# The shifted copy of the attention values made by DMA, with new order words for all engines

## Chip, core and metric

The kernel runs on one core of a Trainium2 chip. The metric is the device time of one execution in microseconds (us). TensorE is written PE, VectorE DVE, ScalarE ACT, GpSimd POOL, and SP is the engine that here only issues DMAs.

## What is computed

Sixteen sequences of 512 tokens by 128 channels pass through a state-space block (Mamba: an input projection, a causal convolution, a scan with 16 states for each of 256 channels, an output projection) and then through two layers of local attention with a feed-forward part. Each block has a layer norm ahead of it and behind it, and a residual. All is in float32.

```python
# state-space block
da = jnp.exp(dt_t[:, :, None] * a);  dbu = dt_t[:, :, None] * b_t[:, None, :] * u_t[:, :, None]
state = da * state + dbu;            y_t = jnp.einsum('bds,bs->bd', state, c_t)
...
# local attention, WINDOW = 64, HEADS = 8, DIM_HEAD = 64: each window looks at itself and the one before
def look_around(t):
    p = jnp.pad(t, ((0, 0), (0, 0), (1, 0), (0, 0), (0, 0)))
    return jnp.concatenate([p[:, :, :w], p[:, :, 1:]], axis=3)
bk, bv = (look_around(bk), look_around(bv))
sim = jnp.einsum('bhwid,bhwjd->bhwij', bq, bk)
...
attn = jax.nn.softmax(sim, axis=-1)
out = jnp.einsum('bhwij,bhwjd->bhwid', attn, bv)
```

## The kernel before

**Streams and rounds.** A batch is one sequence. The work on it is cut into streams: E (entry: norm, input projection, convolution), M (the scan of the state-space block: 32 steps, each a 128x512 scan on DVE), A (front: the first attention layer with its feed-forward part, PSUM banks `f_bank`, SBUF tiles with the number 0) and B (back: the second layer, banks `b_bank`, tiles with the number 1), with small streams F, S and C between them. `program` (L1155) runs rounds. In each, M works on batch k+2, A on k+1, B on k and E on k+3, so that in the rounds 0 to 13 all four run side by side. The order in which an engine issues the pieces of the streams is written out in `ORDER` (L43): a word such as `A2 B1` lets stream A go two pieces on and then B one. `weave` reads it. Every engine executes strictly in its order and waits on semaphores where it must.

**The scan.** Step s of M is four operations: ACT makes `da` by an exponential (L593), POOL makes `dbu` (L645), DVE scans both into `hs` (L617), POOL multiplies by C into `gy` (L662), and PE adds up `y_sum` (L570). `da` is one PSUM bank, so the steps go one by one. The inputs `spread` are read from DRAM by SP in 16 groups (L513, two steps to a group) into three slots. The load of group g waits until step 2(g-3)+1 has been scanned (L512). What bounds the slots is thus the scan itself.

**Attention, first half.** For each of four 128-token tiles q, k and v are projected (L693). DVE turns q and k (`rotate` L885 and L889, `add` L899) and sums squares (L872), ACT squares (L787) and copies, POOL clips the sums (L946) and normalises (L954). For v, `value` in `act_attention` (L790) copies the bank into `w.v` (L796). A tile has two windows, at partitions 0 to 63 and 64 to 127.

**Attention, second half.** A query window needs 128 keys and values that start at a multiple of 64. For the second window of a tile they are the tile itself, `w.v`. For the first window they are the second window of the tile before and the first one of this tile, both in their own partitions. `w.vs` holds them: `vs[0:64, t] = v[0:64, t]` and `vs[64:, t+1] = v[64:, t]`. PE reads both in `value` of `pe_attention` (L728), after it has waited for `v_paired` and `v_before`. `vs` and `v` have a 65th column of ones for each head, whose product is the softmax sum. The tile `vs` serves the feed-forward part as well (`ff`, L1046).

**The copies that the change touches.** ACT copies the upper 64 partitions out of the bank (L795, three for each attention). POOL copies the lower 64 out of `v` (`pair`, L960, four for each attention). DVE writes the ones of the upper partitions with a memset (L902).

**SP.** It issues all loads and stores of the kernel in one queue of its own order. Where it waits for a semaphore, all that stands behind it waits too. `sp_enter` (L344) loads the next x into `sq1[:, 1]` once the back layer's sums of squares have been made (L348).

Of the kernel before, what the change touches and what calls it, by code (L numbers as in the profile page):

```python
# [11 lines left out]
ACT = mybir.ActivationFunctionType  # L12
AX = mybir.AxisListType.X

B, T, D = 16, 512, 128
P = 128
NT = T // P
# [3 lines left out]
DEPTH, HEADS, DH, WIN = 2, 8, 64, 64  # L21
# [26 lines left out]
    "act": (  # L48
# [4 lines left out]
    "dve": (  # L53
# [4 lines left out]
    "pool": (  # L58
        "F4 C1 A4 M1 B1 M1 B1 M2 B1 M1 B1 M2 B1 M1 B3 M1 A1 M1 A2 M1 B1 M1 A1 B1 M1 B2 M1 B1 A1 M2 B1 A1 B2 M4 A3 "
        "M1 A1 M1 A1 M1 A1 M44"),  # L60
    "sp": "M1 F2 M10 E1 M2 C1 M6 B1 M2 S1 M1 S2",
}
# [39 lines left out]
def build(nc, a, out):  # L102
    with ExitStack() as ctx:
# [50 lines left out]
        class Attention:  # L154


            def __init__(self, n, banks, pr):
# [24 lines left out]
                self.turned, self.qk_copied = s("turned", 8), s("qk_copied", 8)  # L182
                self.v_paired, self.v_before = s("v_paired", NT), s("v_before", NT - 1)
                self.scored, self.peaked, self.weighed = s("scored", 4), s("peaked", 8), s("weighed", 8)
# [56 lines left out]
        wf, wb = Attention(0, fa, None), Attention(1, lb, late)  # L241
# [434 lines left out]


        def pe_attention(E, e, b, w, l, x, f):
            for n, take in enumerate(TAKES):
# [48 lines left out]
            def value(hd):  # L728
                E.wait_ge(*w.p_copied(b, hd))
                E.wait_ge(*w.v_paired(b, NT - 1))  # L730
                E.wait_ge(*w.v_before(b, NT - 2))
                if hd:
                    E.wait_ge(*w.o_done(b, hd - 1))
                for p in range(NT):
                    for j in range(2):
                        q0 = p * P + WIN * j
                        op = e.matmul(ot[WIN * j:WIN * j + WIN, p, :], w.p_t[:, hd % 2, q0:q0 + WIN],
                                      (w.vs, w.v)[j][:, p, hd, :], start=True, stop=True)
                op.then_inc(w.valued.sem, 1)
# [29 lines left out]
        def act_attention(E, e, b, w, l):  # L769
# [19 lines left out]
            def value(take):  # L789
                t = int(take[1])  # L790
                E.wait_ge(*w.projected(b, projections.index(take)))
                if w is wb and b > 0 and t == 0:
                    E.wait_ge(*o_made(b - 1))
                if t + 1 < NT:
                    e.activation(w.vs[WIN:, t + 1, :, 0:DH], heads(bank_of(take)[WIN:, :]), ACT.Copy).then_inc(w.v_before.sem, 1)  # L795
                e.activation(w.v[:, t, :, 0:DH], heads(bank_of(take)[:, :]), ACT.Copy).then_inc(w.v_copied.sem, 1)  # L796
# [69 lines left out]
        def dve_attention(E, e, b, w, l, x):  # L866
# [34 lines left out]
            entry = w is wb and b + 2 < B  # L901
            e.memset(w.vs[WIN:, 1:, :, DH:], 1.0)  # L902
            for n in range(8):
# [38 lines left out]
        def pool_attention(E, e, b, w):  # L942
# [13 lines left out]

            def pair(t):

                E.wait_ge(*w.v_copied(b, t))
                e.tensor_copy(w.vs[0:WIN, t, :, :], w.v[0:WIN, t, :, :]).then_inc(w.v_paired.sem, 1)  # L960

            for take in "c0 q0 q1 v0 c1 k0 v1 k1 c2 q2 q3 v2 v3 c3 k2 k3".split():
                if take[0] == "c":
                    clip(int(take[1]))
                elif take[0] == "v":
                    pair(int(take[1]))
                else:
                    normalise(take)
                yield
# [133 lines left out]
        def pool_end(E, e, b):  # L1103
# [4 lines left out]
            yield  # L1108

        def sp_back(E, e, b):  # L1110
            E.wait_ge(*wb.valued(b, HEADS - 1))
            E.wait_ge(*x1_stored(b))
# [64 lines left out]
        with nc.Block() as block:  # L1177
            block.sync(program("sp", dict(C=sp_end, B=sp_back, M=sp_state, F=sp_steps, E=sp_enter, S=sp_spill)))
            block.gpsimd(program("pool", dict(C=pool_end, B=pool_back, A=pool_front, M=pool_state, F=pool_steps)))
# [101 lines left out]
```

## Time and profile before

| | us |
|---|---|
| median of 3 runs (2479.12 to 2483.96) | 2480.55 |
| span of the profiled execution | 2483.7 |
| one round in the middle of the span | 141.0 |
| PE, DVE, ACT, POOL busy in the whole | 1934.9, 1919.8, 1830.6, 1778.2 |

The profiled execution's span is 3.1 us above the median and 0.3 us under the slowest of the three runs. No engine is busy for more than 78% of the span, so an average tells little. A round has stretches with different limits, and rows of its slices are read for that.

### The profile page before, as it was taken

What the parts mean: (1) busy time and instruction counts of PE and PEld (TensorE: products, weight loads), DVE (VectorE), ACT (ScalarE), POOL (GpSimd) and SP (SyncE); (2) the same over time, 40 slices, a digit from 0 to 9 for tenths busy, and PEclk for the clock granted to TensorE, in tenths of its full rate; (3) what the DMA queues carried; (4) which work ended last, traced back from release to release, by engine and by line L of the source; (5) the groups of instructions that cost most, each with busy time, mean ns of one, the idle gap of its engine ahead of it and who ended that gap; (6) DMA issues with size and microseconds to landing.
All of it is one profiled execution on the core that took longest, in us unless ns stands there. A gap on an engine that the chain in (4) does not pass through costs nothing.

```text
span 2483.7 us, 44331 instructions
## 1 busy us (share of the span) xinstructions
PE 1934.9 (78%) x15936; PEld 1113.3 (45%) x15936; DVE 1919.8 (77%) x3509; ACT 1830.6 (74%) x4051; POOL 1778.2 (72%) x1668
## 2 busy tenths in 40 slices
PE   2156788797878888797878879797888879787866
PEld 0013355353635445353635445363645445363634
DVE  3557797978879797988879797988879797977442
ACT  2255788787878878786878878797878878686634
POOL 1969595977959596977959596886959596883020
PEclk9767999999999999999999999999999999999978
DMA  4443423333434333434433333434433333330000
GB/s 163 123 120 98 112 74 104 98 96 103 103 111 104 100 89 95 102 90 115 104 107 95 107 86 91 106 91 116 112 106 95 106 88 91 102 90 9 6 5 9
DMA packets 116107, 231.27 MB, mean 93 GB/s; under 512 B 24880, under 2 KB 57648, under 8 KB 115632
## 3 DMA queue, kind: packets, MB, share of 16 engines
q1 hardware_dynamic: 115888, 228.44, 34.5%
q8 instruction: 126, 2.06, 0.4%
q14 instruction: 93, 0.76, 0.1%
HBM read 185.42 MB, written 42.99 MB: 92 GB/s over the span
## 4 chain that ended last, share of the span: by engine, by line
DVE 30%; PE 28%; ACT 19%; issue 12%; POOL 2%; DMA 1%; DVEq 0%; SPq 0%; POOLq 0%; ACTq 0%
DVE hs L617 9%; DVE m L885 5%; ACT late L850 3%; DVE kr L899 3%; ACT da L593 3%; DVE b_bank L889 3%; PE b_bank L341 3%; DVE f_bank L889 2%; PE b_bank L719 2%; PE f_bank L341 2%; DVE ss L872 2%; PE b_bank L764 2%; DVE mx L916 2%; PE f_bank L995 2%; PE f_bank L1001 2%
## 5 line engine op out<-in xcount | busy, mean ns | idle before, releaser
L617 DVE TENSOR_TENSOR_SCAN hs<-da,dbu 128x512 f32<-128x512 f32 x512 | 622.3, 1215 | 112.8 <-POOL dbu L645 85.4
L662 POOL TENSOR_TENSOR gy<-hs,bc 128x512 f32<-128x512 f32 x512 | 650.4, 1270 | 44.9 <-DVE hs L617 40.9
L645 POOL TENSOR_TENSOR dbu<-spread,bc 128x512 f32<-128x512 f32 x512 | 649.5, 1269 | 9.2 <-DMA spread<-steps 9.2
L593 ACT ACTIVATE da<-spread,rest 128x512 f32<-128x512 f32 x512 | 359.1, 701 | 163.3 <-DVE hs L617 143.9
L954 POOL TENSOR_TENSOR kr<-kr,rn 128x512 f32<-128x512 f32 x256 | 263.6, 1040 | 18.7 <-ACT rn L810 15.3
L693 PE MATMUL b_bank<-rest,h_t 128*128 128x512 f32 x384 | 225.1, 687 | 49.2 <-DVE kr L899 40.8
L693 PE MATMUL f_bank<-rest,h_t 128*128 128x512 f32 x384 | 217.4, 653 | 56.5 <-DVE kr L899 49.3
L570 PE MATMUL y_sum<-gy,rest 128*32 128x512 f32 x1024 | 144.2, 638 | 87.9 <-POOL gy L662 87.9
L341 PE MATMUL b_bank<-first,kr 128*128 128x128 f32 x768 | 131.7, 307 | 97.0 <-DVE kr L899 61.5
L341 PE MATMUL f_bank<-first,kr 128*128 128x128 f32 x768 | 125.1, 291 | 100.3 <-DVE kr L899 63.3
L1107 POOL TENSOR_TENSOR xs<-xs,v 128x512 f32<-128x512 f32 x16 | 18.9, 1184 | 229.6 <-ACT xs L336 229.6
L341 PEld LDWEIGHTS b_bank<-first,kr 128*128 128x128 f32 x768 | 92.1, 154 | 187.3 <-DVE kr L899 145.5
L416 POOL TENSOR_TENSOR k_t<-k_t,m 128x512 f32<-128x512 f32 x32 | 39.9, 1269 | 184.5 <-ACT m L493 184.5
L341 PEld LDWEIGHTS f_bank<-first,kr 128*128 128x128 f32 x768 | 87.2, 146 | 163.3 <-DVE kr L899 108.9
L850 ACT ACTIVATE late<-b_bank,mx 128x128 f32<-128x128 f32 x512 | 139.0, 389 | 25.8 <-DVE mx L916 25.8
L872 DVE TENSOR_REDUCE ss<-sq 128x16 f32<-128x1024 f32 x128 | 154.5, 1207 | 0.0
L850 ACT ACTIVATE sq<-f_bank,mx 128x128 f32<-128x128 f32 x512 | 144.0, 395 | 9.4 <-DVE mx L916 7.8
L693 PEld LDWEIGHTS f_bank<-rest,h_t 128*128 128x128 f32 x384 | 70.8, 205 | 142.5 <-DVE kr L899 77.6
L693 PEld LDWEIGHTS b_bank<-rest,h_t 128*128 128x128 f32 x384 | 71.8, 213 | 121.8 <-DVE kr L899 65.5
L89 ACT ACT_TABLE_LOAD x82 | 105.2, 1283 | 20.2 <-DVE mv_enter L314 7.1
L885 DVE TENSOR_TENSOR m<-f_bank,tab 128x512 f32<-128x512 f32 x128 | 87.2, 681 | 35.3 <-ACT sq L787 35.3
L341 PE MATMUL b_bank<-first,late 128*128 128x128 f32 x512 | 84.6, 289 | 27.3 <-ACT late L850 25.6
(172 smaller groups left out, 4942.1 us busy)
## 6 DMA issues: line engine op xcount, KB each, us to landing
spread<-steps SPq DMA_DIRECT2D x256, 512.0 KB, 4.7
bc<-bc_rows SPq DMA_DIRECT2D x32, 512.0 KB, 6.8
steps<-k_t SPq DMA_DIRECT2D x32, 512.0 KB, 2.7
gate<-gates SPq DMA_DIRECT2D x32, 512.0 KB, 5.6
gates<-kr SPq DMA_DIRECT2D x16, 512.0 KB, 2.7
gates<-late SPq DMA_DIRECT2D x16, 512.0 KB, 3.4
sq<-in_x SPq DMA_DIRECT2D x16, 256.0 KB, 4.8
x<-in_x SPq DMA_DIRECT2D x16, 256.0 KB, 4.8
```

The source lines that it names most:

```text
L341: op = e.transpose(bank[:, n * P:(n + 1) * P], src(n), ident[:, :])
L570: op = e.matmul(y_sum[32 * j:32 * j + 32, :], sel[:, w, :], gy[:, 2 * j + k, :], start=w == 0 and k == 0, stop=w == 1 and k == 1, skip_gro ...
L593: e.activation(da[:, :], spread[:, slot(b, s // 2), 0, :], ACT.Exp, scale=a_neg[:, s:s + 1]).then_inc(decayed.sem, 1)
L617: e.tensor_tensor_scan(hs[:, s % 2, :], da[:, :], dbu[:, s % 2, :], 0.0, ALU.mult, ALU.add).then_inc(scanned.sem, 1)
L645: e.tensor_tensor(dbu[:, s % 2, :], spread[:, slot(b, s // 2), 1, :], bc[:, s % 2, :], ALU.mult).then_inc(fed.sem, 1)
L662: e.tensor_tensor(gy[:, s % 8, :], hs[:, s % 2, :], bc[:, 2 + s % 2, :], ALU.mult).then_inc(read_out.sem, 1)
L693: e.matmul(bank[:, :], w.h_t[:, t * P:(t + 1) * P], wqkv[:, l, part * INNER:(part + 1) * INNER], start=True, stop=True).then_inc(w.project ...
L850: op = e.activation(w.pr[:, hd % 2, p, :], X[hd % 2][:, p * P:(p + 1) * P], ACT.Exp, bias=w.mx[:, hd, p:p + 1])
L872: e.tensor_reduce(w.ss[:, 2 * g:2 * g + 2, :], w.sq[:, :, :].rearrange("p n (h d) -> p n h d", h=HEADS), AX, ALU.add).then_inc(w.summed.se ...
L885: e.tensor_tensor(halves(w.m2[:, n % 2, :]), halves(bank[:, :])[:, :, ::-1, :], table[1], ALU.mult).then_inc(w.rotated.sem, 1)
L889: e.tensor_tensor(halves(bank[:, :]), halves(bank[:, :]), table[0], ALU.mult).then_inc(w.rotated.sem, 1)
L954: e.tensor_tensor(x, x, w.rn[:, n, :].unsqueeze(2).to_broadcast([P, HEADS, DH]), ALU.mult).then_inc(w.normed.sem, 1)
```

## The change

The ACT copy of the upper 64 partitions, the POOL copy of the lower 64 and the DVE memset of the ones go. A new stream part `sp_windows` on SP issues four DMAs from `w.v` to `w.vs` for each attention, two when v tiles 0 and 1 are copied and two when tiles 2 and 3 are. `w.v` has the ones in its 65th column, so they are carried along. `v_paired` now counts the DMAs (2 steps of 32), `v_before` is gone. SP gets a stream A. The order words of all five engines are new.

```diff
-                self.v_paired, self.v_before = s("v_paired", NT), s("v_before", NT - 1)
+                self.v_paired = s("v_paired", 2, 32)
...
+        def sp_windows(E, e, b, w):
+            for i in range(2):
+                E.wait_ge(*w.v_copied(b, 2 * i + 1))
+                e.dma_start(w.vs[0:WIN, 2 * i:2 * i + 2, :, :], w.v[0:WIN, 2 * i:2 * i + 2, :, :]).then_inc(w.v_paired.sem, 16)
+                n = min(2, NT - 1 - 2 * i)
+                e.dma_start(w.vs[WIN:, 2 * i + 1:2 * i + 1 + n, :, :], w.v[WIN:, 2 * i:2 * i + n, :, :]).then_inc(
+                    w.v_paired.sem, 16)
+                yield
...
             def value(hd):
                 E.wait_ge(*w.p_copied(b, hd))
-                E.wait_ge(*w.v_paired(b, NT - 1))
-                E.wait_ge(*w.v_before(b, NT - 2))
+                E.wait_ge(*w.v_paired(b, 1))
...
-                if t + 1 < NT:
-                    e.activation(w.vs[WIN:, t + 1, :, 0:DH], heads(bank_of(take)[WIN:, :]), ACT.Copy).then_inc(w.v_before.sem, 1)
                 e.activation(w.v[:, t, :, 0:DH], heads(bank_of(take)[:, :]), ACT.Copy).then_inc(w.v_copied.sem, 1)
...
-            e.memset(w.vs[WIN:, 1:, :, DH:], 1.0)
...
-            def pair(t):
-
-                E.wait_ge(*w.v_copied(b, t))
-                e.tensor_copy(w.vs[0:WIN, t, :, :], w.v[0:WIN, t, :, :]).then_inc(w.v_paired.sem, 1)
-
-            for take in "c0 q0 q1 v0 c1 k0 v1 k1 c2 q2 q3 v2 v3 c3 k2 k3".split():
+            for take in "c0 q0 q1 c1 k0 k1 c2 q2 q3 c3 k2 k3".split():
...
+        def sp_front(E, e, b):
+            yield from sp_windows(E, e, b, wf)
+
         def sp_back(E, e, b):
+            yield from sp_windows(E, e, b, wb)
             E.wait_ge(*wb.valued(b, HEADS - 1))
...
-    "sp": "M1 F2 M10 E1 M2 C1 M6 B1 M2 S1 M1 S2",
+    "sp": (
+        "M1 F2 M5 A1 M1 B1 M1 E1 B1 M3 A1 M6 C1 M5 S3 B1"),
```

What the new words move is shown at three places of a round. The names have the number 0 for the front and 1 for the back. The changed file is a line or more longer, so the same operation has a slightly higher line number.

**First place, ACT at the start of a round.** Here the norm of the result (`xs`), the first squares (`sq`) and the first value copies (`v`) follow each other. Before:

```order
L787 ACTIVATE sq0<-f_bank0 128x512
L336 ACTIVATE xs1<-xs1,mr_out,rs_out 128x128 x4
L795 ACTIVATE vs0<-f_bank1 64x8x64
L796 ACTIVATE v0<-f_bank1 128x8x64
L787 ACTIVATE sq1<-b_bank0 128x512
L803 ACTIVATE lg0<-ss0 128x16
L810 ACTIVATE rn0<-lg0,columns 128x16
L787 ACTIVATE sq0<-f_bank2 128x512
L795 ACTIVATE vs0<-f_bank0 64x8x64
L796 ACTIVATE v0<-f_bank0 128x8x64
L593 ACTIVATE da<-spread,rest 128x512
L795 ACTIVATE vs1<-b_bank1 64x8x64
```

Now:

```order
L796 ACTIVATE sq0<-f_bank0 128x512
L796 ACTIVATE sq1<-b_bank0 128x512
L337 ACTIVATE xs1<-xs1,mr_out,rs_out 128x128 x4
L803 ACTIVATE v1<-b_bank1 128x8x64
L803 ACTIVATE v0<-f_bank1 128x8x64
L810 ACTIVATE lg0<-ss0 128x16
L817 ACTIVATE rn0<-lg0,columns 128x16
L796 ACTIVATE sq0<-f_bank2 128x512
L810 ACTIVATE lg1<-ss1 128x16
L817 ACTIVATE rn1<-lg1,columns 128x16
```

The back's first value copy (`v1`) has moved up to stand directly behind the norm of `xs1`, ahead of the front's. It waits until POOL has added the residual that it overwrites. The two copies into `vs` are gone.

**Second place, SP in the first half of a round**, from the load of `gate` on. `sq1<-in_x` is the load of the next x. Before:

```order
L516 DMA gate<-gates 128x1024
L513 DMA spread<-steps 128x1x1024 x4
L351 DMA sq1<-in_x 128x4x128
L513 DMA spread<-steps 128x1x1024 x2
L1120 DMA out_dram<-xs0 128x4x128
L513 DMA spread<-steps 128x1x1024 x2
L516 DMA gate<-gates 128x1024
L513 DMA spread<-steps 128x1x1024 x3
L1114 DMA v1<-x1_rows 128x2x64 x4
```

Now:

```order
L682 DMA vs0<-v0 64x1040
L684 DMA vs0<-v0 64x1040
L517 DMA gate<-gates 128x1024
L682 DMA vs1<-v1 64x1040
L684 DMA vs1<-v1 64x1040
L514 DMA spread<-steps 128x1x1024
L352 DMA sq1<-in_x 128x4x128
L682 DMA vs1<-v1 64x1040
L684 DMA vs1<-v1 64x520
L514 DMA spread<-steps 128x1x1024 x3
L682 DMA vs0<-v0 64x1040
```

The load of x stood behind four of the groups (4 to 7) and now stands behind group 4 alone. Two window copies of the back are behind it, and groups 5 to 7 behind those.

On POOL, at the end of the same half. `ss` is a clip, `kr` a normalisation, `vs` the copy of a window, `dbu` and `gy` are steps of the scan. Before:

```order
L954 TENSOR_TENSOR kr0<-kr0,rn0 128x512
L954 TENSOR_TENSOR kr1<-kr1,rn1 128x512 x2
L662 TENSOR_TENSOR gy<-hs,bc 128x512
L645 TENSOR_TENSOR dbu<-spread,bc 128x512
L662 TENSOR_TENSOR gy<-hs,bc 128x512
L645 TENSOR_TENSOR dbu<-spread,bc 128x512
L954 TENSOR_TENSOR kr0<-kr0,rn0 128x512
L960 COPY vs0<-v0 64x520 x2
L662 TENSOR_TENSOR gy<-hs,bc 128x512
L946 TENSOR_SCALAR ss0<-ss0 128x16
L645 TENSOR_TENSOR dbu<-spread,bc 128x512
L954 TENSOR_TENSOR kr0<-kr0,rn0 128x512
```

Now:

```order
L960 TENSOR_TENSOR kr0<-kr0,rn0 128x512
L960 TENSOR_TENSOR kr1<-kr1,rn1 128x512 x2
L663 TENSOR_TENSOR gy<-hs,bc 128x512
L646 TENSOR_TENSOR dbu<-spread,bc 128x512
L663 TENSOR_TENSOR gy<-hs,bc 128x512
L960 TENSOR_TENSOR kr0<-kr0,rn0 128x512
L646 TENSOR_TENSOR dbu<-spread,bc 128x512
L663 TENSOR_TENSOR gy<-hs,bc 128x512
L646 TENSOR_TENSOR dbu<-spread,bc 128x512
L952 TENSOR_SCALAR ss0<-ss0 128x16
L663 TENSOR_TENSOR gy<-hs,bc 128x512
L960 TENSOR_TENSOR kr0<-kr0,rn0 128x512 x2
```

The two copies `vs0` are gone, and a normalisation of `kr0` stands ahead of the `dbu` of step 10 where it stood behind it.

**Third place, DVE in the second half**, around the small operation `mr_enter` of the entry's norm. `rd` and `kr` belong to the attention's results, `hs` is the scan. Before, behind scan step 24:

```order
L922 RECIPROCAL rd0<-f_bank2 128x4
L925 TENSOR_TENSOR kr0<-f_bank2,rd0 128x4x64
L617 SCALAR_TENSOR_TENSOR hs<-da,dbu 128x512
L330 SCALAR_TENSOR_TENSOR mr_enter<-mv_enter,rs_enter 128x4
L922 RECIPROCAL rd0<-f_bank2 128x4
L925 TENSOR_TENSOR kr0<-f_bank2,rd0 128x4x64
L617 SCALAR_TENSOR_TENSOR hs<-da,dbu 128x512
```

Now, behind step 18:

```order
L618 SCALAR_TENSOR_TENSOR hs<-da,dbu 128x512
L928 RECIPROCAL rd1<-b_bank2 128x4
L931 TENSOR_TENSOR kr1<-b_bank2,rd1 128x4x64
L928 RECIPROCAL rd0<-f_bank2 128x4
L331 SCALAR_TENSOR_TENSOR mr_enter<-mv_enter,rs_enter 128x4
L931 TENSOR_TENSOR kr0<-f_bank2,rd0 128x4x64
L618 SCALAR_TENSOR_TENSOR hs<-da,dbu 128x512
```

`mr_enter` is six steps of the scan earlier and stands between two operations of the front's attention.

## Rows read from the trace of the kernel before

**Rows 1.** Slices of one round: length, busy of each engine, granted clock, DMA share.

```profile
core 0: us, PE busy (x) PEld busy (x) DVE busy (x) ACT busy (x) POOL busy (x), PEclk, DMA share, GB/s
...
693.42:703.42 10.00, 10.00 (x33) 4.39 (x34) 6.19 (x19) 8.74 (x17) 1.27 (x1) 1.00 0.44 139
...
713.42:723.42 10.00, 7.02 (x16) 2.48 (x15) 9.96 (x15) 8.44 (x20) 7.41 (x9) 1.00 0.90 210
...
743.42:753.42 10.00, 6.91 (x33) 2.96 (x32) 9.91 (x14) 6.60 (x15) 8.85 (x11) 1.00 0.18 52
...
773.42:783.42 10.00, 9.45 (x171) 6.23 (x163) 9.07 (x21) 10.00 (x30) 10.00 (x9) 1.00 0.50 134
```

**Rows 2.** Groups of instructions by line: count, busy us, mean ns, idle before.

```profile
L960 POOL COPY vs<-v 64x520 f32<-64x520 f32 x128 | 77.5, 612 | 5.3 <-ACT v L796 5.3
...
L795 ACT ACTIVATE vs<-f_bank 64x512 f32<-64x512 f32 x48 | 28.4, 592 | 18.4 <-PE f_bank L693 17.6
...
L902 DVE MEMSET vs<- 64x24 f32 x32 | 2.5, 78 | 2.5
```

**Rows 3.** Timeline of POOL, end of the first half: start, us, [idle before].

```profile
752.78 0.24 POOL L946 TENSOR_SCALAR ss<-ss 128x16 f32<-128x16 f32 x1 [0.21 <-DVE ss L872]
752.99 3.04 POOL L954 TENSOR_TENSOR kr<-kr,rn 128x512 f32<-128x512 f32 x3
...
759.69 1.27 POOL L645 TENSOR_TENSOR dbu<-spread,bc 128x512 f32<-128x512 f32 x1
...
761.91 1.17 POOL L960 COPY vs<-v 64x520 f32<-64x520 f32 x2
763.05 1.26 POOL L662 TENSOR_TENSOR gy<-hs,bc 128x512 f32<-128x512 f32 x1
```

**Rows 4.** Timeline of DVE, the same time.

```profile
751.48 1.21 DVE L872 TENSOR_REDUCE ss<-sq 128x16 f32<-128x1024 f32 x1
...
758.52 1.22 DVE L617 TENSOR_TENSOR_SCAN hs<-da,dbu 128x512 f32<-128x512 f32 x1 [0.93 <-POOL dbu L645]
```

**Rows 5.** Timeline of SP: the issue of groups 5 to 7, then x.

```profile
743.10 11.27 SPq L513 DMA_DIRECT2D spread<-steps  x2
...
760.39 0.53 SPq L351 DMA_DIRECT2D sq<-in_x  x1
```

**Rows 6.** DMA issues by kind: count, KB of one, median us to landing.

```profile
spread<-steps SPq DMA_DIRECT2D x256, 512.0 KB, 4.7
...
sq<-in_x SPq DMA_DIRECT2D x16, 256.0 KB, 4.8
...
x_rows<-x SPq DMA_DIRECT2D x16, 256.0 KB, 2.5
```

**Rows 7.** Groups issued in the burst from 711 to 717 us.

```profile
DMA to landing us min/median/max: 4.6/6.3/9.4
```

**Rows 8.** Slice within that burst, last columns DMA share and GB/s.

```profile
714.50:716.50 2.00, 1.47 (x4) 0.38 (x2) 1.97 (x4) 1.88 (x4) 1.18 (x1) 1.00 1.07 250
```

**Rows 9.** Timeline of DVE around `mr_enter`, one round, the round before, all 13 rounds.

```profile
803.60 3.04 DVE L330 SCALAR_TENSOR_TENSOR mr_enter<-mv_enter,rs_enter 128x4 f32<-128x4 f32 x1
...
663.58 0.57 DVE L330 SCALAR_TENSOR_TENSOR mr_enter<-mv_enter,rs_enter 128x4 f32<-128x4 f32 x1
...
L330 DVE SCALAR_TENSOR_TENSOR mr_enter<-mv_enter,rs_enter x13: 136/3025/3044, 381.7 to 2068.3; 128x4 f32<-128x4 f32 x13
```

**Rows 10.** Timeline of POOL beside the first of these.

```profile
808.39 1.28 POOL L662 TENSOR_TENSOR gy<-hs,bc 128x512 f32<-128x512 f32 x1 [1.78 <-DVE hs L617]
```

**Rows 11.** Timeline of POOL, its last gate in three rounds.

```profile
545.26 1.26 POOL L669 TENSOR_TENSOR gate<-gate 128x512 f32<-128x512 f32 x1 [2.01 <-DVE gate L609]
...
684.93 1.26 POOL L669 TENSOR_TENSOR gate<-gate 128x512 f32<-128x512 f32 x1 [2.01 <-DVE gate L609]
...
826.23 1.26 POOL L669 TENSOR_TENSOR gate<-gate 128x512 f32<-128x512 f32 x1 [2.01 <-DVE gate L609]
```

**Rows 12.** Timeline of POOL, start of the round.

```profile
714.78 1.18 POOL L1107 TENSOR_TENSOR xs<-xs,v 128x512 f32<-128x512 f32 x1 [5.11 <-ACT xs L336]
```

More of the change, by code:

```diff
@@ L44 @@
     "pe": (
[3 rows of a table removed]
[3 rows of a table added]
     "act": (
[4 rows of a table removed]
[4 rows of a table added]
     "dve": (
[4 rows of a table removed]
[4 rows of a table added]
     "pool": (
-        "F4 C1 A4 M1 B1 M1 B1 M2 B1 M1 B1 M2 B1 M1 B3 M1 A1 M1 A2 M1 B1 M1 A1 B1 M1 B2 M1 B1 A1 M2 B1 A1 B2 M4 A3 "
-        "M1 A1 M1 A1 M1 A1 M44"),
-    "sp": "M1 F2 M10 E1 M2 C1 M6 B1 M2 S1 M1 S2",
+        "F4 C1 A2 B1 A1 M2 B1 M2 B2 M3 B1 M1 A1 M1 B1 M1 B1 M1 A1 B1 M2 A1 M2 A1 B1 M1 B1 A1 B2 M3 A1 M3 A1 M1 A2 "
+        "M44"),
+    "sp": (
+        "M1 F2 M5 A1 M1 B1 M1 E1 B1 M3 A1 M6 C1 M5 S3 B1"),
 }
@@ L955, in normalise @@
                                 ALU.mult).then_inc(w.normed.sem, 1)
-            def pair(t):
-                E.wait_ge(*w.v_copied(b, t))
-                e.tensor_copy(w.vs[0:WIN, t, :, :], w.v[0:WIN, t, :, :]).then_inc(w.v_paired.sem, 1)
-            for take in "c0 q0 q1 v0 c1 k0 v1 k1 c2 q2 q3 v2 v3 c3 k2 k3".split():
+            for take in "c0 q0 q1 c1 k0 k1 c2 q2 q3 c3 k2 k3".split():
                 if take[0] == "c":
                     clip(int(take[1]))
-                elif take[0] == "v":
-                    pair(int(take[1]))
                 else:
@@ L1177, in build @@
         with nc.Block() as block:
-            block.sync(program("sp", dict(C=sp_end, B=sp_back, M=sp_state, F=sp_steps, E=sp_enter, S=sp_spill)))
+            block.sync(program("sp", dict(C=sp_end, B=sp_back, A=sp_front, M=sp_state, F=sp_steps, E=sp_enter, S=sp_spill)))
             block.gpsimd(program("pool", dict(C=pool_end, B=pool_back, A=pool_front, M=pool_state, F=pool_steps)))
```

22 rows, old and new, of the table ORDER are left out of this document.

## The prediction

> **What bounds the kernel now.** I read the slices of one round first, then the timelines of the engines where one of them is full, then the queue of SP. A round takes 141.0 us and has three stretches. In the first half (711 to 758 us in the round shown) DVE is full: 9.96 and 9.91 of 10 us [rows 1], while ACT has 8.44 and 6.60. In the second half (from 753 to 824) POOL is full: 10.00 of 10 us from 773 to 783, with DVE at 9.07 [rows 1]. There the scan paces the round: for each step POOL makes one product before it and one behind it. In the tail (825 to 848) PE is full, 10.00 of 10 [rows 1], with the projections and feed-forward products of three streams. So an operation that is taken away helps only if it stands on the engine that is full in its stretch.
>
> **POOL's copies.** 128 copies of 612 ns each go, 77.5 us in all [rows 2], eight in each full round or 4.9 us. Where they stand decides. POOL's last wait of the first half ends at 752.78, on DVE's sum of squares that began at 751.48 [rows 3, 4]. From then on it has no gap for over 30 us. Of the eight copies only the last two stand behind this point: 761.91, 1.17 us for both, directly ahead of the `gy` of step 9 at 763.05 [rows 3]. These 1.17 us are on the path: everything POOL does until the end of the scan comes earlier by them. The other six, 3.7 us, stand where DVE is full, and POOL has to wait for DVE in any case; DVE's work up to that sum of squares is the same set of operations in the new order. Once, at 758.52, DVE had waited 0.93 us for POOL's `dbu` [rows 4], but the normalisations at 752.99 ahead of it stay [rows 3]. The six are worth between 0 and 3.7 us a round; I take 0.1, since 9.91 of 10 leaves no more.
>
> **ACT's copies.** Six a round at 592 ns [rows 2], 3.6 us, all in the first half, where ACT is not full [rows 1]. They are hidden by DVE's work. If DVE were not full they would be worth up to 3.6 us a round. The new words spend a part of it: the back's first value copy now follows the norm of `xs1` directly, and it waits for POOL's residual sum, which began at 714.78 and took 1.18 us when the norm was done [rows 12]. The front's copies, its logarithm and POOL's first normalisations are queued behind that wait, some 1.2 us later. Cover: DVE now has three more rotation pieces ahead of scan step 0, so that step would come about 1.9 us later anyway (three operations of some 0.6 us). Uncovered it costs 1.2 a round. I take 0.
>
> **The memsets.** Two of 78 ns a round on DVE in the full stretch [rows 2]: 0.15 us gained. In the tail the order of PE's products changes and their number does not. PE is full there, so I take 0, with 0.5 to either side.
>
> **The DMAs that come instead.** Eight issues a round. They read `v` and land in `vs`. No window copy is in the old trace. The nearest rows: a store of 256 KB takes 2.5 us from issue to landing, a load of 256 KB 4.8 us [rows 6]; a window pair has 260 KB, or 260 and 130 KB. So 2.5 to 4.8 us, and I take 3. PE reads the back's `vs` first about 15 us after the back's last v copy and the front's over 20 us after the front's, so the transfers are covered. The issue time on SP is 0.4 to 0.5 us each, and SP has room.
>
> **What they are queued with.** The price lies in SP's order. Before, groups 5 and 6 were issued from 743.10 on, and x at 760.39, behind group 7 [rows 5]. Now x stands ahead of groups 5 to 7, and it waits for the back's last sum of squares, 752.6 [rows 4]. Two window copies follow it. So group 5 leaves SP at about 752.6 + 0.5 + 2 x 0.4 = 753.9 in place of 743.1. It lands 4.7 us later if it is alone [rows 6], at 758.6. In the queue are then x, 256 KB, the windows, 390 KB, and itself, 512 KB. In a burst the engines of the DMA were wholly busy at 250 GB/s [rows 8], so these 1158 KB take 4.7 us, and with the 2.6 us that a group needs above its own 2.1 us the landing is at about 752.6 + 4.7 + 2.6 = 759.9. The load of x is slower than its bytes (4.8 us for 256 KB), which may add 1.2: 761.1. Who needs it: ACT's and POOL's step 10. POOL began that `dbu` at 759.69 [rows 3] and now has a normalisation of 1.0 us ahead of it: 760.7. So POOL waits between 0 and 0.4 us by this, and with a landing as late as the longest of the burst, 9.4 us [rows 7], 2.6 us. I take 0.4. The sum without this edit would be 5.6 us better.
>
> The Trainium skill ("SBUF — State Buffer", the section on Door 1) says that a transfer to partitions 0 to 63 reaches only 8 of the 16 ports, and gives 196 GB/s against 328 GB/s for all partitions. It speaks against these copies: by it the 390 KB would take 2.0 us, not 1.6, an estimate, and the sum would be 5.6 us worse. No row here shows a copy of half the partitions by itself.
>
> **`mr_enter`.** This DVE operation on 4 columns takes 3.04 us in one round and 0.57 us in the round before [rows 9]. In the long case it ends when POOL runs dry at 806.6, and POOL's next product then starts 1.78 us late [rows 10]. The price in the round is read from POOL's last gate: 139.67 us from 545.26 to 684.93 with the short one, 141.30 to 826.23 with the long one [rows 11]. Of 13 such operations, between 136 and 3044 ns with a median of 3025 [rows 9], 8 are long, and a long one costs some 1.3 us a round. The new place, behind step 18, has the same dense POOL beside it, so I take no change. If the six-steps-earlier place is always short, 8 x 1.3 = 10 us are gained; if it is always long, 5 x 1.3 = 6.5 us are lost. The skill's page "SBUF — State Buffer" (SBUF: two separate sides) has the rule: a DVE operation with two SBUF inputs and a POOL operation exclude each other for a whole instruction. `mr_enter` reads two SBUF tiles, and the trace agrees.
>
> **The sum.** A full round: -1.17 - 0.1 - 0.15 + 0.4 = -1.0 us. There are 14 full rounds (0 to 13): -14 us. The rounds before and behind them have no front copies beside the scan, or no scan; there ACT's copies may give up to 1 us, and I take 0. The profiled execution would go from 2483.7 to 2469.7. It has span 3.1 above the median; the three runs differ by 4.8 us, as a few more or fewer long `mr_enter` would. From the median 2480.55 the forecast is 2466.5.
>
> **The rivals.**
> Group 5 eats the gain. The window copies and x slow each other, POOL's step 10 waits 1.0 to 1.4 us. For it: the landing times of the burst, 6.3 us in the middle [rows 7], would mean 760.2 to 761.5 and more with x. Against it: the burst had 2.5 MB in flight, here it is 1.2. Then -1.17 - 0.25 + 1.2 = -0.2 a round: 2477.
>
> Group 5 comes late, slower. If it lands at 763.3 (9.4 us from its issue, the longest of the burst), POOL waits 2.6 us: +1.2 a round, +17: 2497. It decides from a landing of 762.1 on, where the wait of 1.4 us has used up the gain. ACT, which stands at the same group with its `da`, then holds the back's first exponentials too.
>
> A larger gain. POOL's freed time lets steps run ahead, and `mr_enter` is short in its new place: -14 - 10 = 2456. For it: five rounds of 13 were short by chance. Against it: POOL is as full at step 18 as at step 24.
>
> The change doesn't do what it says: no chance worth a number, the order shows `vs` written by DMA alone.
>
> **How the numbers follow.** Forecast 0.50 (2462 to 2474), group 5 eats the gain 0.20 (2474 to 2484), slower 0.15 (2486 to 2500), larger gain 0.15 (2450 to 2461). What a measurement of this kernel can tell from no change is about 0.2%, 5 us. Faster by more than that, under 2475.6: the first and the last case, 0.65. Within: the second, 0.20. Slower: 0.15. The range leaves out the far halves of the outer cases: 2453 to 2487.
>
> **What would show it.** In the profile after: POOL busy 77 us less, ACT 57 less; the round at about 140.0 us; the slices of the first half with DVE still at 9.9 and POOL lower; in the second half POOL still at 10. SP's issue of group 5 at about 42 us behind the round's first DVE rotation, its landing 6 to 7 us later, and a wait of POOL's `dbu` or ACT's `da` on `spread` under 0.5 us a round (the rival: 1 to 1.4 us, in nearly all rounds). The forecast is wrong if DVE is not full in the first half, so that the six copies count, if the tail grows, or if PE waits for `vs`.

## The result, and the profile after

| | us |
|---|---|
| before, median of 4 runs (2478.51 to 2483.96) | 2479.84 |
| after, median of 4 runs (2459.03 to 2466.45) | 2461.09 |
| ratio, with its 95% interval | 0.992 [0.9905, 0.9935] |
| span of the profiled execution, before and after | 2483.7, 2459.8 |

The change gains 18.8 us. The forecast was 2466.5 with a range of 2453 to 2487, so the number held. Its reasons held much less, so that the number held in part by luck, and most of this part is about that.

The busy line of the page after, against 1934.9, 1919.8, 1830.6 and 1778.2 before:

```profile
PE 1893.9 (77%) x15808; PEld 1114.3 (45%) x15936; DVE 1892.7 (77%) x3477; ACT 1778.1 (72%) x3955; POOL 1711.4 (70%) x1540
```

POOL is busy for 66.8 us less (128 instructions fewer; the forecast had 77), ACT for 52.5 less (96 fewer; the forecast had 57). Those 119 us of work bought 19.

Slices of one round after, at the same distance from the round's first rotation as those of [rows 1] (columns: length, busy of PE, PEld, DVE, ACT, POOL, granted clock, DMA share, GB/s):

```profile
686.87:696.87 10.00, 10.00 (x29) 3.85 (x28) 6.38 (x20) 8.62 (x16) 1.27 (x1) 1.00 0.46 153
706.87:716.87 10.00, 6.91 (x16) 2.67 (x15) 10.00 (x17) 6.62 (x17) 5.55 (x7) 1.00 0.84 201
736.87:746.87 10.00, 5.99 (x24) 3.08 (x23) 8.65 (x12) 6.10 (x14) 9.16 (x9) 0.94 0.01 2
766.87:776.87 10.00, 8.91 (x159) 5.94 (x162) 9.69 (x21) 9.84 (x29) 9.79 (x8) 1.00 0.39 101
```

The tail (first line) is full on PE as before. At the start of the round DVE is full, at the end of the first half it is not: 8.65 of 10, where [rows 1] have 9.91. (In the mean of the eleven rounds below it is 9.0 against 9.9.) In the second half DVE has risen from 9.07 to 9.69 and POOL has fallen from 10.00 to 9.79. POOL's last gate, against [rows 11]:

```profile
680.28 1.26 POOL L670 TENSOR_TENSOR gate<-gate 128x512 f32<-128x512 f32 x1 [2.86 <-DVE gate L610]
820.08 1.26 POOL L670 TENSOR_TENSOR gate<-gate 128x512 f32<-128x512 f32 x1 [2.86 <-DVE gate L610]
```

This round takes 139.8 us; before, one took 139.67 or 141.30.

**Where in the round.** From the same rows of the timelines I took four stretches in eleven full rounds of every kernel, those in which M scans batches 4 to 14 (k from 2 to 12). The tail runs from `gy` 31 to the first rotation (the first of DVE's turns of q and k for the next front attention), the first half from there to scan 9 on DVE, the middle on to `gy` 20 on POOL, the end on to `gy` 31. Means in us; "long" counts the `mr_enter` above 2 us among 13; "drain" is what lies behind the last gate.

| kernel | round | tail | first half | scan 9 to `gy` 20 | `gy` 20 to 31 | long | drain |
|---|---|---|---|---|---|---|---|
| before | 140.51 | 29.44 | 47.19 | 35.74 | 28.14 | 8 | 254.1 |
| after | 139.64 | 28.70 | 48.01 | 35.86 | 27.07 | 0 | 246.1 |
| after, again (e8) | 139.65 | 28.71 | 47.94 | 35.95 | 27.05 | 0 | 245.9 |
| copies alone (e1) | 139.96 | 29.41 | 46.79 | 35.73 | 28.04 | 6 | 253.0 |
| words alone (e2) | 142.24 | 28.71 | 49.96 | 36.55 | 27.02 | 0 | 248.7 |
| `mr_enter` moved (e3) | 140.01 | 29.44 | 47.16 | 36.10 | 27.31 | 0 | 253.0 |
| `mr_enter` by columns (e4) | 139.95 | 29.44 | 47.30 | 35.74 | 27.47 | 0 | 255.8 |
| ACT's copies only (e5) | 140.13 | 29.41 | 46.80 | 35.75 | 28.16 | 7 | 253.1 |
| POOL's last two only (e6) | 139.91 | 29.45 | 47.18 | 35.75 | 27.54 | 2 | 254.7 |
| POOL's other six only (e7) | 140.38 | 29.45 | 47.27 | 35.75 | 27.91 | 4 | 252.8 |
| e1, steps 10 and 11 reordered (e12) | 140.18 | 29.41 | 46.96 | 35.73 | 28.08 | 7 | 254.6 |
| after, x behind group 7 (e9) | 139.06 | 28.70 | 47.80 | 35.52 | 27.05 | 0 | 242.0 |
| after, `mr_enter` back (e10) | 142.42 | 28.70 | 47.48 | 35.47 | 30.77 | 9 | 246.3 |
| after, `mr_enter` by columns (e11) | 139.84 | 28.71 | 48.55 | 35.54 | 27.05 | 0 | 246.4 |

A profile is one execution. The number of long `mr_enter` differs from one to the next, so the column "`gy` 20 to 31" is to be read together with "long". The columns of the scan repeat within 0.1 us (after and e8). The drain repeats less well: kernels that have the old words there lie between 252.8 and 255.8.

The round lost 0.87 us, 9.6 in eleven rounds. The three first rounds give 6.5, the last 1.0, the drain 8.0, and the first gate stands 1.3 later. Together that is the 23.9 us between the spans. So 9.6 us of them are in the rounds that the table takes apart, and what the first rounds gained was not taken apart.

### The profile page after: what moved, and what is told of

Its sections match the earlier page's. It is cut to its first block, busy times and chain, and to the rows that moved or that the text cites. A ratio compares the mean times of both kernels' runs of the same rounds, so it can differ in the third digit from the quotient of the medians.

```text
span 2459.8 us, 44075 instructions
## 1 busy us (share of the span) xinstructions
PE 1893.9 (77%) x15808; PEld 1114.3 (45%) x15936; DVE 1892.7 (77%) x3477; ACT 1778.1 (72%) x3955; POOL 1711.4 (70%) x1540
## 4 chain that ended last, share of the span: by engine, by line
PE 38%; DVE 23%; ACT 13%; issue 9%; POOL 8%; DMA 4%; SPq 0%; DVEq 0%; POOLq 0%; ACTq 0%
DVE hs L618 6%; DVE m L892 4%; PE f_bank L342 4%; PE b_bank L342 4%; DVE kr L906 3%; POOL gy L663 3%; DMA spread<-steps 3%; POOL dbu L646 3%; ACT da L594 3%; PE b_bank L703 3%; PE f_bank L746 3%; PE y_sum L571 2%; DVE b_bank L896 2%; PE b_bank L773 2%; DVE ss L879 2%
## 5 line engine op out<-in xcount | busy, mean ns | idle before, releaser
L342 PE MATMUL b_bank<-first,kr 128*128 128x128 f32 x768 | 123.7, 296 | 57.8 <-DVE kr L906 41.8
L342 PEld LDWEIGHTS f_bank<-first,kr 128*128 128x128 f32 x768 | 93.3, 151 | 146.4 <-DVE kr L906 70.4
L90 ACT ACT_TABLE_LOAD x82 | 105.2, 1283 | 20.4 <-DVE mv_enter L315 7.3
L892 DVE TENSOR_TENSOR m<-b_bank,tab 128x512 f32<-128x512 f32 x128 | 87.2, 681 | 30.6 <-ACT sq L796 30.6
```

Of the source, the lines that this page charges most:

```text
L90: self.e.preload_act_table_set(name)
L342: op = e.transpose(bank[:, n * P:(n + 1) * P], src(n), ident[:, :])
L892: e.tensor_tensor(halves(w.m2[:, n % 2, :]), halves(bank[:, :])[:, :, ::-1, :], table[1], ALU.mult).then_inc(w.rotated.sem, 1)
```

## The experiments

### The two halves of the change, each alone

e1 keeps the words of before (SP's gets places for the windows) and takes the DMAs for all copies. e2 takes the new words and keeps the copies on ACT and POOL.

```diff
 e1: -  e.activation(w.vs[WIN:, t + 1, ...]) on ACT, e.tensor_copy(w.vs[0:WIN, t, ...]) on POOL, e.memset(w.vs[WIN:, 1:, ...]) on DVE
     +  sp_windows, as in the change; "sp": "M1 F2 M7 A1 B1 M2 B1 M1 A1 E1 M2 C1 M6 B1 M2 S1 M1 S2"
 e2: -  ORDER of before for pe, act, dve, pool, sp
     +  ORDER of after, without the places of the windows; each pair(t) on POOL directly behind a normalisation
```

> The window copies are made by DMA, and every other instruction stands in the order of the kernel before (empty pieces where POOL's copies were; SP issues the front's and the back's first pair behind group 4, the back's second behind group 6, the front's second behind group 7). Theory of the prediction: the two copies of 1.17 us ahead of step 9's gy and the memsets are gained in 14 rounds, so 16 to 20 us less than before, with mr_enter long in some rounds as before. Rival (the new words make the gain): within 5 us of before. If the drain's 8 us come from the copies, the part behind the last scan shortens by 3 us or more; else it stays.

> The new order words with the old copies (each POOL copy directly behind the normalisation that stood ahead of it, ACT's two copies in one piece). Theory of the prediction: the words give the shorter mr_enter, up to 10 us, and change the tail by 0.7 us a round, while the POOL copies stay on the path: 5 to 15 us less than before. Rival (words make the gain): 15 us or more. Third case: the words are made for free engines, and with the copies in place they lose: slower than before by up to 10 us.

e1: 2478.83 us (before 2481.47), ratio 0.9995 [0.9987, 1.0004]. No gain. e2: 2502.05 us, ratio 1.0082 [1.007, 1.0095]. 20 us slower. Neither half is worth anything, and together they gain 0.8%. Where POOL's copies stand in e2 is my choice, one of several, so the 20 us belong to this placement. In the table the words gain 0.7 us in the tail, and about 1.1 at the end since no `mr_enter` is long, but they cost 2.8 in the first half and 0.8 in the middle as long as the copies are there. The DMAs then take 1.95 and 0.69 of that back. That these words were laid out for engines without copies is my reading of it. At the end of the first half of e2, POOL and then DVE:

```profile
754.40 1.04 POOL L941 TENSOR_TENSOR kr<-kr,rn 128x512 f32<-128x512 f32 x1
755.39 1.17 POOL L947 COPY vs<-v 64x520 f32<-64x520 f32 x2
756.53 1.26 POOL L632 TENSOR_TENSOR dbu<-spread,bc 128x512 f32<-128x512 f32 x1
```

```profile
759.09 0.69 DVE L872 TENSOR_TENSOR m<-f_bank,tab 128x512 f32<-128x512 f32 x1 [0.74 <-ACT sq L774]
...
763.50 1.22 DVE L604 TENSOR_TENSOR_SCAN hs<-da,dbu 128x512 f32<-128x512 f32 x1 [1.13 <-POOL dbu L632]
```

DVE has gaps here that end on ACT and on POOL. Under the new words it no longer covers their copies. That holds from the start of the round on, where [rows 1] have DVE at 9.96. The slice of e2:

```profile
715.32:725.32 10.00, 6.63 (x15) 2.48 (x14) 9.28 (x14) 7.58 (x17) 4.96 (x7) 1.00 0.85 196
```

Without the copies (after, the slice from 706.87) it is 10.00 again.

### Which copies are worth something under the old words

> The kernel before with only ACT's copies (upper 64 partitions) made by DMA; POOL's stay, the order is the old one. Theory of the prediction: DVE hides ACT in the first half, so within 4 us of before (2 us from the memsets). Rival: ACT's copies delay the squares and the banks that DVE waits for, 0.5 us a round or more: 7 us or more less.

> The kernel before with only the last two of POOL's eight copies of a round (the front's tiles 2 and 3, ahead of step 9's gy) made by one DMA. Theory: these two are the ones on the path: 14 x 1.17 = 16 us less. Rival (all eight count alike): a quarter of the effect of e1.

> The kernel before with the other six of POOL's eight copies made by DMA and the last two left on POOL. Theory: they stand where DVE is full, so 0 to 3 us less. Rival: POOL's six copies of 3.7 us a round delay the norms and products that DVE needs: 10 us or more less.

```diff
 e5: ACT's copies by DMA and DVE's memsets gone, POOL's stay
 e6: POOL's pair(2) and pair(3) of the front by DMA, all else stays
 e7: POOL's other six by DMA, all else stays
```

e5: 2478.95, ratio 0.9981 [0.9972, 0.999]. e6: 2480.22, 0.9994 [0.9982, 1.0005]. e7: 2484.74, 1.0007 [0.9998, 1.0017]. So the step with the largest term in the forecast, POOL's last two copies, gives nothing, and the run without ACT's copies, which I had at 0, is the only one with a gain. The table has it at 0.39 us a round (47.19 to 46.80), which is 5 us in 14 rounds; the ratio says 4.7. The two memsets, which I had at 0.15, went with them in e5, and no run parts the two. The gain is small beside the noise between sessions: before took 2482.91 us in this one and 2486.66 in that of e12, on the same chip, and e1, whose profile has the same shorter first half (46.79), shows no gain in time.

POOL in e1 at steps 9 and 10, where [rows 3] have the two copies:

```profile
758.45 1.28 POOL L663 TENSOR_TENSOR gy<-hs,bc 128x512 f32<-128x512 f32 x1
760.00 0.25 POOL L962 TENSOR_SCALAR ss<-ss 128x16 f32<-128x16 f32 x1 [0.27 <-DVE ss L889]
760.21 1.27 POOL L646 TENSOR_TENSOR dbu<-spread,bc 128x512 f32<-128x512 f32 x1
761.98 1.04 POOL L970 TENSOR_TENSOR kr<-kr,rn 128x512 f32<-128x512 f32 x1 [0.50 <-ACT rn L825]
762.98 1.27 POOL L663 TENSOR_TENSOR gy<-hs,bc 128x512 f32<-128x512 f32 x1
```

The `gy` of step 9 does come 1.13 us earlier behind its scan (3.39 us in place of 4.52). Then POOL stands still and waits for DVE's last sum of squares and for the `rn` that ACT makes from it. From scan 9 to `gy` 20 it takes 35.74 us before and 35.73 in e1.

### Is it these two waits, or what lies behind them?

e12 is e1 with steps 10 and 11 laid out as in the new words, and nothing else:

```diff
 DVE:  m f_bank
-      ss(front 3) hs(10)
+      hs(10) ss(front 3)
 POOL: gy(9)
-      ss dbu(11) kr gy(10) kr dbu(12)
+      dbu(11) ss gy(10) kr kr dbu(12)
 ACT:  -  q_t lg da(11) rn
       +  da(11) q_t lg rn
```

> The kernel of the copies alone (all copies by DMA, old words) with one place in the words changed: the scan of step 10 on DVE stands ahead of the front's last sum of squares instead of behind it, POOL makes the dbu of step 11 ahead of the clip of that sum and the gy of step 10 ahead of the normalisation, and ACT's exponential of step 11 moves up past one copy and one logarithm. Nothing else. Theory: with the copies alone POOL reached its gy of step 9 1.13 us earlier, but then stood 0.27 us for DVE's sum of squares and 0.50 us for ACT's rn behind it, which gave 0.86 us back at step 10 of every round. With the step's own work in between, the gy of step 11 should start about 57.4 us behind the first rotation instead of 58.2, the two waits should go, and the round should be 0.7 us shorter: about 2469 us against 2478.8 for the copies alone. Rival: the first half is bounded by DVE here, and what POOL gains is lost at the next operation in any case (the scan of step 11 stands behind two maxima on DVE); then the time is that of the copies alone, 2478 to 2480 us, and the new words owe their gain to the tail and the end of the kernel.

2481.44 us against 2486.66 for before, ratio 0.9974 [0.9964, 0.9984]. Its theory needed 0.7 us a round. The rows of POOL:

```profile
757.95 1.28 POOL L653 TENSOR_TENSOR gy<-hs,bc 128x512 f32<-128x512 f32 x1
...
760.82 1.27 POOL L653 TENSOR_TENSOR gy<-hs,bc 128x512 f32<-128x512 f32 x1
...
765.27 1.29 POOL L653 TENSOR_TENSOR gy<-hs,bc 128x512 f32<-128x512 f32 x1
...
767.98 1.27 POOL L653 TENSOR_TENSOR gy<-hs,bc 128x512 f32<-128x512 f32 x1 [0.19 <-DVE hs L608]
```

The `gy` of step 11 stands 57.5 us behind the first rotation (707.77), as the theory had it, and not 58.2. The gain is gone one step later: POOL waits for the scan. DVE in e1 and e12 at that scan (rotations at 708.27 and 707.77):

```profile
766.53 0.18 DVE L938 RECIPROCAL rd<-b_bank 128x4 f32<-128x4 f32 x1 [0.54 <-PE b_bank L756]
...
767.17 1.22 DVE L618 TENSOR_TENSOR_SCAN hs<-da,dbu 128x512 f32<-128x512 f32 x1
```

```profile
766.04 0.18 DVE L928 RECIPROCAL rd<-b_bank 128x4 f32<-128x4 f32 x1 [0.54 <-PE b_bank L746]
...
766.68 1.22 DVE L608 TENSOR_TENSOR_SCAN hs<-da,dbu 128x512 f32<-128x512 f32 x1
```

Scan 12 starts 58.90 and 58.91 us behind the rotation. It stands behind the back's attention on DVE, which waits for PE's value product. So the theory falls and the rival stands: up to here DVE, with ACT and PE in its chain, sets the pace, and what POOL gains is lost at scan 12. The middle is 35.73 us again. The ratio is about 0.2% below that of e1, which ran on another chip, and the profile shows no stretch that is shorter (a round takes 140.18 us against 139.96); where that difference comes from stays open.

The trace of before had told it. This is POOL just behind the 30 us without a gap:

```profile
785.19 1.28 POOL L662 TENSOR_TENSOR gy<-hs,bc 128x512 f32<-128x512 f32 x1 [0.21 <-DVE hs L617]
...
788.11 1.27 POOL L662 TENSOR_TENSOR gy<-hs,bc 128x512 f32<-128x512 f32 x1 [0.40 <-DVE hs L617]
```

Ahead of the `gy` of steps 17 and 18 POOL waits for DVE. What it saves before that point can only lengthen these waits, as long as DVE does not come earlier. From step 18 on I take POOL to set the pace: it has no gap up to `mr_enter`, and now DVE waits for it (scan 21):

```profile
796.80 1.22 DVE L617 TENSOR_TENSOR_SCAN hs<-da,dbu 128x512 f32<-128x512 f32 x1 [0.71 <-POOL dbu L645]
```

The page had a hint too, in its chain of work that ended last, here before, then after:

```profile
DVE 30%; PE 28%; ACT 19%; issue 12%; POOL 2%; DMA 1%; DVEq 0%; SPq 0%; POOLq 0%; ACTq 0%
```

```profile
PE 38%; DVE 23%; ACT 13%; issue 9%; POOL 8%; DMA 4%; SPq 0%; DVEq 0%; POOLq 0%; ACTq 0%
```

POOL had 2% of it. I had not looked. It is a hint and no proof: under the old words this share lies between 2% (before, e3, e6) and 11% (e1), with the same 35.7 us from scan 9 to `gy` 20 in before, e6 and e1. What decides is e6.

### `mr_enter`

e3 moves it in the kernel of before to its new place (behind step 18, its `rs_enter` on ACT with it). e10 does the reverse in the kernel after, with the two steps that hang on it (the norm on ACT, the padding on DVE). e4 and e11 leave it in its place, in before and after, and change its form (e11 that of the small norm operations of all blocks, not of `mr_enter` alone):

```diff
 e4, e11:
-            e.scalar_tensor_tensor(w.mr[:, :], w.mv[:, :, 0], -1.0, w.rs[:, :], ALU.mult, ALU.mult)
+                for t in range(NT):
+                    op = e.tensor_scalar(w.mr[:, t:t + 1], w.mv[:, t, 0:1], w.rs[:, t:t + 1], -1.0, ALU.mult, ALU.mult)
 e3:  DVE: - hs(24) mr_enter rd      + hs(18) ... rd0 mr_enter kr0 hs(19)
 e10: DVE: - rd0 mr_enter kr0 hs(19) + hs(24) mr_enter rd ... ; the padding behind it
```

> The kernel before with mr_enter alone moved from behind scan step 24 to its place in the changed kernel, between two operations of the front's attention behind step 18 (and the exponential that feeds it moved up on ACT). Theory: mr_enter is short (0.8 us) in all rounds, and 8 long ones at 1.3 us are gained: 10 us less. Rival: the place is as good as the other, POOL's products are as dense: mr_enter is long in about half of the rounds, within 4 us.

> The kernel before with mr_enter made by four DVE operations of one column, each with one tensor input and a scalar from SBUF, in the same place. Theory (the long mr_enter waits because it reads two SBUF tensors while POOL works): the four take under 0.4 us in all, no wait, 8 x 1.3 = 10 us less. Rival (the wait belongs to the place or to the norm's data, not to the form): the first of the four takes up to 3 us as before, no gain.

> The changed kernel with mr_enter put back behind scan step 24 (and what hangs on it, the pad's memset and the norm on ACT, moved behind it). Theory (its place is worth what the long ones cost): mr_enter is long, 2 to 3 us, in half of the rounds or more: 7 to 15 us above e8. Rival: short here as well, since POOL and DVE stand to each other in another phase: within 4 us of e8.

> The changed kernel with all five small norm operations of two SBUF inputs (mr_enter, mr_ff, mr_x, mr_out) made by four operations of one column and one tensor input. Theory: the 0.8 us of mr_enter and the 0.4 to 0.6 of mr_ff become 0.3 each, without a wait for POOL: 0 to 6 us under e8, which would be the fastest of all. Rival: four operations cost more than one where POOL is idle (in the tail), 0 to 3 us above e8.

e3: 2477.12, ratio 0.9989 [0.998, 0.9998]. e4: 2478.15, 0.9987 [0.9979, 0.9996]. e10: 2503.21, 1.0074 [1.0057, 1.0091]. e11: 2463.09, 0.9913 [0.99, 0.9926]. The operation after (with POOL beside it), by columns in e4, and in e10 with the POOL product behind it:

```profile
782.91 0.80 DVE L331 SCALAR_TENSOR_TENSOR mr_enter<-mv_enter,rs_enter 128x4 f32<-128x4 f32 x1
```

```profile
782.41 1.28 POOL L663 TENSOR_TENSOR gy<-hs,bc 128x512 f32<-128x512 f32 x1 [0.41 <-DVE hs L618]
783.64 1.27 POOL L646 TENSOR_TENSOR dbu<-spread,bc 128x512 f32<-128x512 f32 x1
```

```profile
799.22 0.55 DVE L332 TENSOR_SCALAR mr_enter<-mv_enter,rs_enter 128x1 f32<-128x1 f32 x4
```

```profile
952.68 3.56 DVE L323 SCALAR_TENSOR_TENSOR mr_enter<-mv_enter,rs_enter 128x4 f32<-128x4 f32 x1
```

```profile
958.00 1.27 POOL L655 TENSOR_TENSOR gy<-hs,bc 128x512 f32<-128x512 f32 x1 [1.79 <-DVE hs L610]
```

In its new place it is short in every one of the 13 rounds, 0.80 us (0.83 in one), and ends where POOL goes from one instruction to the next. In the old place it waits for up to three POOL instructions. Why it is let in at the first boundary here and not there, no run settles. In the new place it always begins 0.5 us into a `gy` ahead of which POOL has waited for DVE. In the old one of before it begins beside a `dbu` at the same 0.7 us in the long cases and in some of the short ones (803.60 and 663.58 in [rows 9]). The four one-column operations, which read one tensor and a scalar from SBUF and not two tensors, took 0.55 us in all rounds in the same place beside the same dense POOL. The Trainium skill ("SBUF — State Buffer", SBUF: two separate sides) says that a DVE operation with two SBUF inputs and a GpSimd operation that reads SBUF hold the ports they share in turn, each for its whole instruction, while the other is blocked. The trace agrees in that `mr_enter` with two tensors ends where a POOL instruction ends and in the form with one tensor does not wait. In e10 it was also passed over at two such ends (1.1 and 2.3 us after its start, of 3.56), so the block lasted longer than the one instruction that was under way. In the old words the worth is small: e3 saves 0.83 us at the end and gives 0.36 back in the middle, where it now stands in DVE's chain with 0.83 us; in time 2 to 3 us. In the new words the old place is dear: the end takes 30.77 us in place of 27.05, 41 us in all with its two companions, so that the changed kernel without this one move is slower than the kernel before. After the change the form is of no use: 0.58 us in place of 0.80, and the time (e11, with the other norms changed as well) is that of after within 2 us.

### The queue of SP

> The changed kernel again, to be the base of the three others on this chip: 0.992 of before.

> The changed kernel with the load of x moved on SP from ahead of the spread groups 5 to 7 to behind them (and behind the back's second windows). Theory: group 5 lands about 1.5 us earlier, ACT's wait for it of 0.6 us a round goes, and nothing else, since POOL and DVE did not wait for it: within 3 us of e8. Rival: the late group pushes ACT's exponentials and so the second half: 5 us or more under e8.

```diff
 e9: "sp":
-        "M1 F2 M5 A1 M1 B1 M1 E1 B1 M3 A1 M6 C1 M5 S3 B1"
+        "M1 F2 M5 A1 M1 B1 M1 B1 M3 E1 A1 M6 C1 M5 S3 B1"
```

e8 is the kernel after once more: 2461.77, ratio 0.9906 [0.9893, 0.9919]. e9, on the same chip, has the load of x behind group 7: 2450.67 us, ratio 0.9869 [0.9854, 0.9883]. It is 11.1 us faster than the kernel after and the fastest of all. SP after, then in e9 (three groups are one row):

```profile
747.13 0.38 SPq L352 DMA_DIRECT2D sq<-in_x  x1
747.55 0.52 SPq L682 DMA_DIRECT2D vs<-v  x1
748.11 0.60 SPq L684 DMA_DIRECT2D vs<-v  x1
748.75 5.91 SPq L514 DMA_DIRECT2D spread<-steps  x3
```

```profile
740.25 0.46 SPq L681 DMA_DIRECT2D vs<-v  x1
740.76 0.60 SPq L683 DMA_DIRECT2D vs<-v  x1
741.40 10.34 SPq L513 DMA_DIRECT2D spread<-steps  x3
751.84 0.54 SPq L351 DMA_DIRECT2D sq<-in_x  x1
```

With the first rotation at 704.86 and 703.15, group 5 goes out 43.9 us behind it after, and 38.3 in e9. ACT's exponential of step 10 after:

```profile
754.76 0.69 ACT L594 ACTIVATE da<-spread,rest 128x512 f32<-128x512 f32 x1 [0.59 <-DMA spread<-steps]
```

In e9, in this round, it does not wait. Over the eleven rounds this wait has a mean of 0.42 us after and of next to nothing in e9. The rounds are 0.59 us shorter (against e8): 0.43 in the middle, 0.14 in the first half. Over the whole scan it is 5.9 us, and the drain is 3.9 shorter, which one profile of each does not make firm. So about half of the 11.1 us is explained by the rounds.

## The prediction, point by point

**DVE is full in the first half, POOL in the second, PE in the tail.** Half right. DVE with its chain holds on to step 18, not to 753. The step that failed is the sentence on the last two copies: "These 1.17 us are on the path: everything POOL does until the end of the scan comes earlier by them." I read that POOL had no gap for 30 us and took this for proof that it sets the pace. The wait for DVE came 2 us behind the end of what I had read. The term of -1.17 a round measured 0.0 (e6).

**The other six, and ACT's.** Under the old words the six are worth nothing (e7), as forecast. ACT's were 0 in the sum and, with the memsets that the sum had at -0.15, measured -0.39 a round (e5). But both were costed against the old cover. Under the new words all copies together are worth 2.6 us a round (142.24 to 139.64, with the placement of e2), and DVE is not full there; which of the copies count was not tried. The condition was written down ("If DVE were not full"), and again among the signs that the forecast is wrong. The slices show it met: 9.28 of 10 in e2 and 8.65 after.

**The tail.** Taken as 0, with 0.5 to either side: "PE is full there, so I take 0". It gained 0.74 us, in every run with the new words. That the number of PE's products does not change was right: from `gy` 31 to the first rotation there are 20 feed-forward products (L992, L995) before and after. Their order changed. PE before, then after:

```profile
825.38 1.12 PE L435 MATMUL b_bank<-m,first 128*128 128x512 f32 x2
826.34 1.02 PE L992 MATMUL b_bank<-h_t,rest 128*114 128x512 f32 x2
...
829.94 1.12 PE L435 MATMUL b_bank<-m,first 128*128 128x512 f32 x2 [0.34 <-ACT kr L476]
```

```profile
818.47 1.11 PE L991 MATMUL b_bank<-h_t,rest 128*114 128x512 f32 x2
819.42 1.02 PE L436 MATMUL b_bank<-m,first 128*128 128x512 f32 x2
820.28 1.02 PE L994 MATMUL b_bank<-h_t,rest 128*114 128x512 f32 x2
...
824.22 1.02 PE L436 MATMUL b_bank<-m,first 128*128 128x512 f32 x2
```

The gates stand at 826.23 and 820.08. One pair has moved ahead of the gate, which comes 0.85 us later behind `gy` 31, since DVE has one feed-forward product of 0.75 us ahead of it. That is no gain by itself. PE was not full behind the gate: it waited 0.34 us for ACT's `kr` at 829.94, and after the change it doesn't. From the last `y_sum` product to the first one that reads `vs` the way is 0.63 us shorter (17.79 to 17.16), with this wait in it; what the order of the products gives of the rest was not taken apart. The other part is on ACT. It made `lv_out` ahead of the first square, for which the first rotation waits, and now makes it behind. ACT before, then after:

```profile
850.83 0.28 ACT L321 ACTIVATE lv_out<-mv_out,columns 128x4 f32<-128x4 f32 x1
...
851.75 0.60 ACT L787 ACTIVATE sq<-f_bank 128x512 f32<-128x512 f32 x1
```

```profile
844.03 0.60 ACT L796 ACTIVATE sq<-f_bank 128x512 f32<-128x512 f32 x1
844.52 0.29 ACT L322 ACTIVATE lv_out<-mv_out,columns 128x4 f32<-128x4 f32 x1
```

From PE's first `xs` product to the rotation it is 3.70 us in place of 3.90.

**`mr_enter`.** Taken as no change, with a rival in which it is always short. The rival came true, 0.80 us in all rounds; its price of 10 us was too high for the old words (2 to 3 us, e3) and nearer for the end of the round after (28.14 to 27.07, that is 1.07 a round). Which of the words give that end besides the place of `mr_enter` was not tried.

**ACT's start of the round.** The forecast had the back's first value copy wait up to 1.2 us for POOL's residual sum. Of ACT's waits ahead of its value copies after, those for that sum (us, times):

```profile
POOL xs L1106: 20.3, 15
```

That is 1.35 each. The cover was smaller than forecast: scan step 0 starts 11.96 us behind the first rotation in place of 10.56, 1.4 later and not 1.9. The words' loss in the first half (+0.82 net) holds this and the waits of DVE for ACT's squares; how much is whose was not taken apart.

**The window copies and group 5.** The kinds of DMA after, of 260 and of 130 KB:

```profile
vs<-v SPq DMA_DIRECT2D x96, 260.0 KB, 5.9
...
vs<-v SPq DMA_DIRECT2D x32, 130.0 KB, 4.5
```

I had taken 3 us from a bound of 2.5 to 4.8; it is 5.9, above the bound, and nothing waits for it. By how much their going to half the partitions slows them can't be told, for they travel beside loads. Group 5 was forecast at 42 us behind the rotation with a landing 6 to 7 us later; it was 43.9, and the groups issued there landed after 6.0 to 7.2. ACT's `da` is the one that waits, and POOL's `dbu` does not. The term was +0.4 a round; e9 shows 0.59.

**The drain.** Taken as 0. It is 8.0 us shorter, by one profile each, 5.4 of it with the words alone and 1.1 with the copies alone. 3.7 us of it lie between the last gate and the last front's first rotation: 20.3 to 20.4 us in every kernel with the new words, 24.0 to 24.1 in every one with the old. The rest stays open.

**The sum.** -1.0 was forecast for a round and -0.87 measured, by other terms: tail -0.74, first half +0.82, middle +0.12, end -1.07. The forecast was right within 5.4 us because what it credited to two copies came from places it had at nothing. That is luck. From span to span it had -14 us (2483.7 to 2469.7) and the profiles show -23.9, of which the drain, forecast at nothing, is 8.0.

## To carry to other kernels

A run without gaps on an engine does not make it the bound: read on to its next wait for another engine, since what is saved before it goes into that wait. Its share of the chain that ended last is a hint, and a run with that one saving alone decides. A change that frees an engine and a new order are one change: costed apart, each against the old schedule, both came out at nothing or worse, and the gain was in the two together. In a queue, a load that waits for something late belongs behind the loads that are needed first: one place in SP's order was worth 11 us here, more than half of what the whole change gained; the rounds show 5.9 of them.

## What the hardware showed that I had not expected

A DVE operation on 4 columns with two SBUF inputs took between 0.14 and 3.75 us beside POOL's stream, and at the same 0.7 us into a POOL instruction 0.57 us in one round and 3.04 in another. As four one-column operations with a scalar operand it took 0.55 us in all 13 rounds (e4). A copy of 260 KB from SBUF to SBUF, into 64 partitions, took 5.9 us at the median to land, where a store of 256 KB took 2.4 in the same profile.
